# Cross attention of layer 0: heads in parts of TensorE's array, softmax sums by TensorE, and the largest score subtracted on GpSimd

## The reference

```python
def _L0_xattn_ref(query, key_value, Wq, bq, Wk, bk, Wv, bv, Wo, bo):
    scale = D ** (-0.5)
    q = (query @ Wq + bq).reshape(B, Nq, H, D).transpose(0, 2, 1, 3)
    k = (key_value @ Wk + bk).reshape(B, Nkv, H, D).transpose(0, 2, 1, 3)
    v = (key_value @ Wv + bv).reshape(B, Nkv, H, D).transpose(0, 2, 1, 3)
    attn = jnp.einsum('bhqd,bhkd->bhqk', q, k) * scale
    attn = jnp.clip(attn, -CLAMP, CLAMP)
    attn = jax.nn.softmax(attn, axis=-1)
    x = jnp.einsum('bhqk,bhkd->bqhd', attn, v).reshape(B, Nq, Cq)
    return x @ Wo + bo
...
x = _layernorm(x + _L0_attn_ref(...), axis=-1)
x = _layernorm(x + _L0_xattn_ref(x, ctx_768, ...), axis=-1)
```

## Time and profile before

| | us |
|---|---|
| median of 3 runs (lowest, highest) | 2505.74 (2503.68, 2508.46) |
| the profiled execution | 2505.45 |
| its span | 2503.4 |
| DVE busy / PE busy / ACT busy / POOL busy | 1900.6 / 1849.5 / 1337.7 / 801.1 |
| preparation for cross0 | 654 to 698 |
| cross0, its steady part | 744 to 1075 |

### The profile page before, as it was taken

The page is one execution under the profiler, slowest core; times in us unless marked ns, Lnnn a source line. Parts: engine busy times, 40 slices in busy tenths (PEclk is TensorE's granted clock), DMA queues, the critical chain, the costliest instruction groups (busy, mean ns, idle before and its releaser), DMA issues. The chain is left out here.

```text
span 2503.4 us, 35555 instructions
## 1 busy us (share of the span) xinstructions
PE 1849.5 (74%) x11696; PEld 1181.1 (47%) x11696; DVE 1900.6 (76%) x4634; ACT 1337.7 (53%) x3303; POOL 801.1 (32%) x889
## 2 busy tenths in 40 slices
PE   8849999999658888874555554785999999344555
PEld 4413333333346776763444443453777767133333
DVE  4678888887358888878999997433666665599998
ACT  2106666667313433430688889649888852133333
POOL 2510000000026346423333331002633643355553
PEclk9959999999779999996766666677999999667666
DMA  2011111110010100000000000200000000000000
GB/s 73 17 27 29 30 29 28 30 30 17 22 43 11 30 11 10 11 1 1 1 1 1 1 1 1 65 1 17 1 18 1 1 1 1 32 13 13 13 13 17
DMA packets 42805, 41.50 MB, mean 17 GB/s; under 512 B 16054, under 2 KB 34670, under 8 KB 42622
## 3 DMA queue, kind: packets, MB, share of 16 engines
q1 hardware_dynamic: 42622, 39.23, 5.9%
HBM read 22.03 MB, written 4.19 MB: 10 GB/s over the span
## 5 line engine op out<-in xcount | busy, mean ns | idle before, releaser
L763 ACT ACTIVATE ST<-ST,aexp 128x1 f32<-128x1 f32 x2046 | 582.7, 374 | 53.5 <-PEq L57 53.5
L597 ACT ACTIVATE PT<-PS 128x512 f32<-128x512 f32 x576 | 309.8, 597 | 219.3 <-PE PS L482 188.2
L558 DVE CUSTOM_DVE_ANT_0 junk<-PS,maskw 128x128 bf16<-128x128 f32 (+3 forms) x512 | 226.4, 486 | 33.8 <-PE PS L459 33.8
L459 PE MATMUL PS<-KT,QT 48*128 48x512 bf16 (+3 forms) x768 | 190.2, 351 | 54.1 <-DMA QT<-QS 33.0
L94 PE MATMUL PS<-ident,X 128*128 128x128 f32 x320 | 76.3, 326 | 188.3 <-DVE X L128 171.0
L94 PE MATMUL PS<-ident,j_t 128*128 128x128 f32 x320 | 77.1, 426 | 165.6 <-ACT j_t L1800 136.6
L561 DVE TENSOR_REDUCE MX<-PS 128x1 f32<-128x512 f32 x256 | 164.6, 684 | 27.7 <-PE PS L459 24.8
L501 PE MATMUL PS<-PT,VP 128*32 128x256 f32 (+1 forms) x2560 | 184.2, 370 | 0.0
L1561 PE MATMUL PS<-L_xattn_VW,l_pT 112*128 112x256 f32 x704 | 159.4, 382 | 9.3 <-DVE i_xb L1587 6.5
L123 POOL TENSOR_TENSOR n_rs<-n_ve,neghalf 128x1 f32<-128x1 f32 x96 | 110.3, 1165 | 153.4 <-DVE n_ve L118 153.4
L459 PEld LDWEIGHTS PS<-KT,QT 48*128 48x128 bf16 x768 | 58.5, 94 | 199.9 <-issue 80.4
(11 more groups left out here) (297 smaller groups left out, 4500.4 us busy)
## 6 DMA issues: line engine op xcount, KB each, us to landing
KT<-KS SPq DMA_DIRECT2D x192, 32.0 KB, 2.0
QT<-QS SPq DMA_DIRECT2D x192, 32.0 KB, 2.0
xs<-in_x SPq DMA_DIRECT2D x8, 512.0 KB
cx<-in_x SPq DMA_DIRECT2D x32, 128.0 KB, 2.0
out<-j_xn SPq DMA_DIRECT2D x32, 128.0 KB, 1.7
QT<-NMT SPq DMA_DIRECT2D x192, 2.0 KB
f_raw<-in_L_ffn_w SPq DMA_DIRECT2D x2, 1024.0 KB, 5.2
j_raw<-in_L_ffn_w SPq DMA_DIRECT2D x2, 1024.0 KB, 5.1
```

Of the source, the lines that this page charges most:

```text
L459: T.matmul(bank(u % 3)[:, 0:w * P], QT[i % R][rows, qt * P:(qt + 1) * P], KT[i % R][rows, k0 * P:(k0 + w) * P], start=True, stop=True).the ...
L558: V.tensor_tensor_reduce(junk[u % 3][:, 0:w * P], bank(u % 3)[:, 0:w * P], maskw[:, BANK - w * P:], 1.0, NEG, ALU.add, ALU.max, MX[i % 2][ ...
L597: C.activation(PT[n % 4][:, 2 * pr + e, 0:w], bank(3 + u % 3)[:, 0:w], ACT.Exp, scale=0.25).then_inc(e_done, 1)
L763: C.activation(self.ST[:, m, t:t + 1], self.ST[:, m, t - 1:t] if t else self.zero[:, :], ACT.Tanh, bias=self.BU[:, m, t:t + 1], scale=self ...
```

## The change

Six things in one edit, all in cross attention 0.

1. **Scores.** `KX` holds each group of four heads apart: 64 rows (four heads of 16) by 4 x 77 = 308 columns, for two blocks of 128 rows. A matmul uses 64 rows of the array, and the two groups of a block stand in different rows. The four matmuls become five (308, 308, 308, 154, 154 columns), which write to three banks; the last one shares a bank with the first and waits for it (`d_first`).
2. **Clip.** Two instructions, one for 924 and one for 308 columns.
3. **Subtraction.** POOL subtracts the largest score, behind `d_xb` and ahead of `nD`'s root.
4. **Sums.** DVE's sum and reciprocal of 16 columns and POOL's product with them are gone; the transposes of `d_s` are made from the exponentials as they are. PE multiplies them with ones as well, into the second half of bank 7, so that each of the 128 rows and columns has the sum that belongs to its head.
5. **PV.** In place of 12 matmuls with 128 weight columns there are 18 with 32 (two heads), four of them in different column parts of the array, and 18 more for the sums.
6. **Division.** ACT's copy of `aT` is gone. DVE takes the reciprocal of the sums (128x256, out of PSUM) and multiplies PV's result with it into `d_aT`; this stands behind the apply of `nC`. PE's `wo` waits for it.

The preparation is one stage in place of two: both projections follow each other (values first), the values are expanded for two heads at a time (308 columns) into one of two buffers, PE turns them in pieces of 32 rows, 18 for each batch and 18 for the ones, and ACT makes all copies of these.

```diff
+        PLACE = {0: 0, 1: 1, 6: 2, 2: 3, 3: 4, 7: 5, 4: 6, 5: 7}
+            self.pairs = [(q, g) for q in range(KD) for g in range(4)]
+            self.start = {pair: self.PLACE[4 * pair[0] + pair[1]] * self.wdt for pair in self.pairs}
+            self.meets = [(i, q, g) for g in range(4) for q in range(KD) for i in range(VN)
+                          if self.start[q, g] < (i + 1) * VR and self.start[q, g] + self.wdt > i * VR]
...
+            def pe():
...
+                for w_, landed_, b0, done in ((wv, v_in, 4, v_proj), (wk, k_in, 2, k_proj)):
+                    T.wait_ge(landed_, 32)
+                    for j in range(KD):
+                        for k, n in cw:
+                            last = T.matmul(bank(b0 + j)[:, 0:B * NCTX], w_[0:n, k, j * P:(j + 1) * P], ctxT[0:n, k, :],
+                                            start=k == 0, stop=k == 1)
+                        last.then_inc(done, 1)
+                for b in range(B + 1):
+                    T.wait_ge(vx_done, b + 1)
+                    if b == 1:
+                        T.wait_ge(k_done, KD)
+                    if b >= 2:
+                        T.wait_ge(v_copy, 4 * (b - 1))
+                    for k in range(5):
+                        for g in range(4):
+                            if k < len(self.of_g[g]):
+                                i, q, _ = meets[self.of_g[g][k]]
+                                rows, c0 = slice(32 * g, 32 * g + 32), VR + i * VR - self.start[q, g]
+                                last = T.transpose(bank(TURNED[b % 2][g])[0:VR, 32 * k:32 * k + 32], VX[b % 2][rows, q, c0:c0 + VR],
+                                                   ident[rows, rows])
...
+        SCORES = [(0, 0, 308, 0, 0), (BANK, 0, 308, 0, 1), (2 * BANK, 0, 308, 1, 0), (BANK + 308, 154, 154, 1, 1), (308, 0, 154, 1, 1)]
...
+                    for at, k0, n, q, g in SCORES:
+                        rows = slice(64 * g, 64 * g + 64)
+                        if (at, q) == (308, 1):
+                            T.wait_ge(d_first, sc + 1)
+                        last = T.matmul(PS[:, at:at + n], qT[sc % 2][rows, q * P:(q + 1) * P], x.KX[rows, q, sc % B, k0:k0 + n],
+                                        start=True, stop=True)
...
-                            last = T.matmul(bank(7)[:, q * P:(q + 1) * P], x.VB[:, n, o % B, :],
-                                            pT[o % 2][:, i * P:(i + 1) * P], start=n == of_q[0][0], stop=n == of_q[-1][0])
+                    for to, of in ((0, o % B), (D, B)):
+                        for q in range(nblk):
+                            of_g = [[(n, i) for n, (i, *pair) in enumerate(x.meets) if pair == [q, g]] for g in range(4)]
+                            for k in range(3):
+                                for g in range(4):
+                                    if k < len(of_g[g]):
+                                        n, i = of_g[g][k]
+                                        last = T.matmul(bank(7)[32 * g:32 * g + 32, to + q * P:to + (q + 1) * P], x.VB[:, n, of, :],
+                                                        pT[o % 2][:, i * P:(i + 1) * P], start=k == 0, stop=k == len(of_g[g]) - 1)
...
-                    V.tensor_reduce(den[p % 4][:, :], by_head(s[p % 4][:, :]), AX.X, ALU.add).then_inc(d_den, 1)
-                    V.wait_ge(d_den, p + 1)
-                    V.reciprocal(den[p % 4][:, :], den[p % 4][:, :]).then_inc(d_rden, 1)
...
-                    V.tensor_sub(by_head(s[sc % 4][:, :]), by_head(s[sc % 4][:, :]), over_keys(mx[sc % 4])).then_inc(d_sub, 1)
...
+                if on(o):
+                    V.wait_ge(d_o, o + 1)
+                    V.reciprocal(den[o % 2][:, :], bank(7)[:, D:2 * D]).then_inc(d_den, 1)
+                    V.wait_ge(d_den, o + 1)
+                    V.tensor_mul(aT[o % 2][:, :], bank(7)[:, 0:D], den[o % 2][:, :]).then_inc(d_aT, 1)
...
-                if on(o):
-                    C.wait_ge(d_o, o + 1)
-                    C.copy(aT[o % 2][:, :], bank(7)[:, 0:D]).then_inc(d_aT, 1)
...
-                    G.tensor_tensor(by_head(s[p % 4][:, :]), by_head(s[p % 4][:, :]), over_keys(den[p % 4]), ALU.mult).then_inc(d_p, 1)
...
+                if on(sc):
+                    G.wait_ge(d_mx, sc + 1)
+                    G.tensor_tensor(by_head(s[sc % 4][:, :]), by_head(s[sc % 4][:, :]), over_keys(mx[sc % 4]), ALU.subtract).then_inc(d_sub, 1)
```

More of the change, by code:

```diff
@@ L1073, in cross_layer0 @@
     def cross_layer0(XQ, RS, w1, w2, R):
[L1074 to L1075 removed]
+        x = PairedCross()
+        x.prepare()
         ctx, st = x.ctx, Stage(nc, "cross0")
[L1077 removed]
+        nblk, bo, bcol = x.nblk, x.bo, x.bcol
         cx, oT = ring(ctx, "cx", 2, [P, D]), ring(ctx, "c_oT", 2, [P, D])
@@ L1080, in cross_layer0 @@
         xb, s = ring(ctx, "d_xb", 4, [P, D]), ring(ctx, "d_s", 4, [P, SC])
-        mx, den = ring(ctx, "d_mx", 4, [P, H0]), ring(ctx, "d_den", 4, [P, H0])
+        mx, den = ring(ctx, "d_mx", 4, [P, H0]), ring(ctx, "d_den", 2, [P, D])
         pT = ring(ctx, "d_pT", 2, [VR, VN * P])
         et, eq, dsc = ring(ctx, "e_t", 2, [P, D]), ring(ctx, "e_xq", 2, [P, D], BF16), ring(ctx, "e_dsc", 2, [P, P])
+        d_first, = st.sems("d_first")
         x_in = st.slots("x_in", 2)
         c_tr, c_oT, c_mm, c_xb, c_y, c_xn = st.sems("c_tr c_oT c_mm c_xb c_y c_xn")
-        d_tr, d_xT, d_q, d_qT, d_xb, d_sc, d_clip, d_mx, d_sub, d_exp, d_den, d_rden, d_p, d_ptr, d_pT = st.sems(
-            "d_tr d_xT d_q d_qT d_xb d_sc d_clip d_mx d_sub d_exp d_den d_rden d_p d_ptr d_pT")
+        d_tr, d_xT, d_q, d_qT, d_xb, d_sc, d_clip, d_mx, d_sub, d_exp, d_den, d_ptr, d_pT = st.sems(
+            "d_tr d_xT d_q d_qT d_xb d_sc d_clip d_mx d_sub d_exp d_den d_ptr d_pT")
         d_o, d_aT, d_mm, d_y, d_xn = st.sems("d_o d_aT d_mm d_y d_xn")
@@ L1137, in pe @@
                         T.wait_ge(d_clip, sc)
[L1138 to L1144, removed]
+                    for at, k0, n, q, g in SCORES:
[4 more added lines that the diff above has]
+                                        start=True, stop=True)
+                        if at == 0:
+                            last.then_inc(d_first, 1)
                     last.then_inc(d_sc, 1)
@@ L1173, in pe @@
                         T.wait_ge(d_y, o)
-                    for q in range(nblk):
-                        of_q = [(n, i) for n, (i, jj) in enumerate(x.meets) if jj == q]
-                        for n, i in of_q:
-                            last = T.matmul(bank(7)[:, q * P:(q + 1) * P], x.VB[:, n, o % B, :],
-                                            pT[o % 2][:, i * P:(i + 1) * P], start=n == of_q[0][0], stop=n == of_q[-1][0])
+                    for to, of in ((0, o % B), (D, B)):
+                        for q in range(nblk):
+                            of_g = [[(n, i) for n, (i, *pair) in enumerate(x.meets) if pair == [q, g]] for g in range(4)]
+                            for k in range(3):
+                                for g in range(4):
+                                    if k < len(of_g[g]):
+                                        n, i = of_g[g][k]
+                                        last = T.matmul(bank(7)[32 * g:32 * g + 32, to + q * P:to + (q + 1) * P], x.VB[:, n, of, :],
+                                                        pT[o % 2][:, i * P:(i + 1) * P], start=k == 0, stop=k == len(of_g[g]) - 1)
                     last.then_inc(d_o, 1)
```

112 lines of the change are left out of this document (103 added, 9 removed).

## The result

| | before | changed |
|---|---|---|
| median (lowest to highest), us | 2505.26 (2503.68 to 2508.46), 4 runs | 2525.78 (2525.33 to 2527.22), 4 runs |
| profiled execution / its span | 2505.45 / 2503.4 | 2525.69 / 2524.0 |
| mean granted clock | 0.838 | 0.827 |

The ratio is 1.0076, 95% interval 1.0061 to 1.0091: the change makes the kernel 0.8% slower. 2522 was forecast.

The account below looks back on a forecast made before the run. DVE was taken to bound the steady part, PE close behind; the change makes one loop over both. 2505.45 − 16 (preparation) − 1.6 (chain) + 5 (fill, drain) + 29 (clock) = 2521.9, so 2522; range 2485 to 2560.

Parts of the forecast that it names:

- The reciprocal: DVE's reciprocal of 256 columns, between PE's outputs and `wo`: 1.85 us, at 6.7 ns a column.
- The cheap rival: Reciprocal takes only 0.41, the step's chain falls to 10.7 and the clock holds: 2451 us; chance 0.13.
- The estimate worked out from it: Eight passes a column at 0.96 GHz make the reciprocal 2.13 us, and the kernel some 10 us slower.
- The chain of a step: To apply 3.23, apply 0.73, reciprocal 1.88, product 0.54, `wo` and transposes 2.92, scores 1.42, clips 1.42: 12.14 against 12.20.
- a fall: TensorE's granted clock at its lower level, 1.2 GHz, for 3.4 us after a PE gap: 1.6 us lost each.
- The clock: PE's new wait ahead of `wo` lowers the granted clock in two of three steps: +29 us.
- The gap: PE idles some 2.6 us in every step, waiting for `aT` ahead of `wo`.
- the loop: 27 steady steps of cross0 over DVE and PE: −1.6 from the chain, +29 from the clock.
- Two thirds: Share of the 27 steps taken to lose 1.6 to the clock; 3 of 8 gives +16, all +43.
- The preparation: Keys and values: both projections end at 670.0, transposes 10, stage ends at 682.3: −16, range −20 to −5.
- Fill and drain: Two last tiles +2 each, four steps at either end 0.3 more: +5 us in all.
- Beside the path: PV 2.2 instead of 2.92, on no path; POOL's 2.25 subtraction covered by reciprocal and product; uncovered, up to 2.25 a step.

Follow-up runs that it names:

- rec16: Changed kernel with the reciprocal taken of 16 of the 256 columns and the product made with these 16, repeated; 2453.55 us, ratio 0.9783.
- fill14: Changed kernel with 14 identity transposes issued by PE in each step ahead of its wait for DVE's product; 2487.32 us, ratio to before 0.9917.
- fullrows: Changed kernel with the five scores' matmuls over all 128 rows, `KX` expanded with zeros; 2531.89 us, ratio 1.0094.
- early3: Changed kernel with sums first, reciprocal and product behind `nC`'s statistics, quantiser's largest magnitude behind `nD`'s, POOL's subtraction ahead of its root of `nC`; 2441.86 us, ratio 0.9738.
- prepseq: Changed kernel with the 90 transposes of the preparation ordered by row part, those of one part behind each other; 2524.53 us, ratio 1.0074.
- pvseq: Changed kernel with the 36 matmuls of PV ordered one column part after another, not going round the four parts; 2515.41 us, ratio 1.004.
- subdve: Changed kernel with the subtraction of the largest score back on DVE, behind the largest score, in place of POOL's; 2577.69 us, ratio 1.0276.
- early: Changed kernel with PE's sums made first, into bank 2, and reciprocal and product right behind the largest score on DVE; 2538.94 us, ratio 1.0124.
- early2: Changed kernel with PE's sums first, reciprocal and product behind `nC`'s statistics, quantiser's largest magnitude for the next tile behind `nD`'s; 2466.63 us, ratio 0.9836.

## Why the prediction was right

- **The reciprocal.** 1.85 forecast, from 0.25 for 16 columns and 0.15 for one; measured 1.75. The cheap rival (0.41) is out: 16 columns take 0.24 (rec16) and 256 columns 1.75, 6.3 ns a column. The Trainium skill, "VectorE: DVE Perf Modes", section "First, the fixed hardware budget", has the reciprocal as an iterative divide with a repeat count of 8. The estimate worked out from it, 2.13, was too long: at the 0.96 GHz of that estimate the measured slope is six cycles a column and not eight.
- **The chain of a step.** 12.14 forecast; a step without a fall is 11.84. In the order of the forecast's sum a step of fill14 has 3.16 (forecast 3.23), 0.72 (0.73), 1.78 (1.88), 0.48 (0.54), 2.87 (2.92), 1.41 (1.42) and 1.42 (1.42): every term is right or a little high. Inside the scores' 1.41 the split was off: they took 1.37, not 1.25, and the clip started 0.04 behind them, not 0.17. That steps with POOL's work on the weights come out like the others is so in fill14 (11.84 to 11.88).
- **The clock.** The mechanism is shown by fill14. The gap is 2.1, where 2.6 was forecast. A fall costs 1.67 (1.6 forecast). With 22 of them gone the 27 steps are 36.2 shorter, where I took 18 falls; the loop is 34.5 longer, 27.4 forecast. Two thirds was a choice between 3 of 8 and all, and it was low; 24 of 27 steps had one. fullrows shows that the count depends on more than the gap.
- **The preparation** is the term that was mis-sized: −21.7 for −16, outside its own range of −20 to −5. The two projections follow each other as reckoned (669.93 for 670.0). The five rounds of transposes took 4.3 to the last one's end, where I took 10, between 5.5 and 21. Both bounds came from transposes that move 128 columns; these move 32 (`32x32` in the rows above, `128x128` in the earlier trace rows) and take 0.036 to 0.041 each.
- **Fill and drain**, +5 forecast: −2.65 and +7.7, 5.1 together. A step of the fill takes 17.24 and is counted in the loop. In it PE waits 3.86 for ACT's copy `c_oT`, which stands behind the exponential, and that behind POOL's subtraction; I had not seen this one. In early3, with the subtraction earlier, the step is 12.4; but it is 12.36 in rec16 and 13.85 in prepseq, with the subtraction where it was, so how much of the 17.24 is its doing stays open.
- **Beside the path.** PV took 2.39 (2.2 forecast) and is covered, as pvseq shows. POOL's subtraction was off the loop, as subdve shows. That it holds no operation of DVE was true only of this order: rec16, early and early2 have an `e_t` of 1.53 and 2.15 and an apply of 1.64 beside it, early3 has none. What was held are operations of DVE between two places in SBUF, each until POOL's was over; the reciprocal out of PSUM was not. The Trainium skill, "SBUF — State Buffer", section "SBUF: two separate sides", has the pair of ports that DVE and POOL share as a lock, which one of them keeps for its whole instruction while the other stands still; all four traces agree.

The misses went against each other: −5.7 in the preparation, +7.1 in the loop, +2.7 in the rest of the program, for which I had nothing. That the total came out 4 us from the forecast is in part their doing.

## What to carry to other kernels

Before work is taken off the busiest engine, look for the loop it is part of: here DVE's work fell by 0.64 us a step (292.6 and 275.25 us in 27 steps) and the step became longer, since what it gained stood between two pieces of PE's work. Where PE waits in every step of a pipeline, ask what its clock does behind the wait, and test it with work that nobody reads; when an edit's effect is small or has the wrong sign, repeat it with the clock held. A long operation of POOL on SBUF is best placed beside an operation of DVE that reads PSUM: that was early3 against early2, 25 us.

## What the runs showed of the hardware

- The same gap of 2.1 us ahead of `wo` was followed by a fall in 23 of the 26 steps behind the fill's in the changed kernel, and in 15 of 26 in fullrows; one of 1.84 in 17 of 26 (pvseq, where two of the gaps are 1.71 and 1.46, and an 18th fall is behind a wait ahead of the weights' sum); those of 0.58 (fill14) and 0.68 (early2, early3) in none of the plain steps.
- A fall cost 1.67 a step where it lay on `wo`, the transposes and the scores (changed kernel), and 0.00 to 0.52 where it lay on PV (kernel before, those of 3.4 us).
- The order in which four column parts or row parts are used hardly matters: 72 records of 128 columns took 2.39 going round the parts and 2.66 one part after the other; 36 transposes of 32 rows took 1.48 and 1.62.
- Two row parts of 64 rows beside each other: the scores took 1.37, and 2.24 over 128 rows (fullrows).
- POOL's subtraction of 2.25 to 2.30 us in SBUF held DVE's SBUF-to-SBUF operations until 0.15 us after its end (rec16, early, early2), and did not hold the reciprocal out of PSUM (early3).
- DVE's reciprocal costs 6.3 ns a column between 16 and 256 columns, against 1.16 for the sum over 1232 columns (1.43).
